# Layer-norm statistics of five stages taken in the tail of the stage ahead, in a one-core transformer kernel

## The reference

```
x = x + L0_xattn(_layernorm(x), ctx, ...)   # a0: 32 heads, position bias, own rms norm
x = x + L0_ffn(_layernorm(x), ...)          # f0: 512x512 base, 8 LoRA experts with a sparsemax router
x = x + L1_xattn(_layernorm(x), ctx, ...)   # a1: attention inside patches, 8 heads
x = x + L1_ffn(_layernorm(x), ...)          # int8 matmul, done inside stage a2
x = x + L2_xattn(_layernorm(x), ctx, ...)   # a2: 32 query, 8 key heads, rotary positions
x = x + L2_ffn(_layernorm(x), ...)          # f2: gated, 1376 wide, weights rounded to 4-bit codes
x = x + L3_xattn(_layernorm(x), ctx, ...)   # a3: keys from context and x, normed queries and keys
x = x + L3_ffn(_layernorm(x), ...)          # f3: 64 experts of rank 8, best 16 of them
```

## Time and profile before

| | us |
|---|---|
| median of 3 runs (3140.70 to 3143.68) | 3140.89 |
| the profiled execution | 3129.63 |
| its span, first to last instruction | 3127.9 |
| first VectorE instruction of f0 | 905.84 |
| of a1 | 988.94 |
| of f2 | 1894.89 |
| of a3 | 2112.50 |
| of f3 | 3012.56 |

### The profile page before, as it was taken

How to read it: one execution, slowest core, us unless ns; L and a number is a source line. 1 busy time by engine, 2 the same in 40 slices (tenths; PEclk the granted TensorE clock), 3 DMA queues, 4 the chain that set the end, 5 groups by cost and what they waited for, 6 DMA issues and landing times. The chain is left out here.

```text
span 3127.9 us, 44736 instructions
## 1 busy us (share of the span) xinstructions
PE 2876.8 (92%) x16404; PEld 2478.2 (79%) x16404; DVE 1994.3 (64%) x3493; ACT 1376.1 (44%) x3393; POOL 1322.3 (42%) x1178
## 2 busy tenths in 40 slices
PE   7999999999876886969999998998999999999967
PEld 6888888888765764758888886877999999999946
DVE  5777777778765787878988875345444444444453
ACT  3656556565521553234444432214434444443520
POOL 6455535544422653455555540004434434343420
PEclk9999999999987997989999999999999999999978
DMA  4112112112121002011111103101000101000000
GB/s 134 46 58 64 59 44 64 60 50 65 39 82 46 11 4 65 27 40 43 40 41 41 39 21 115 41 11 41 28 18 28 28 18 29 27 28 18 17 28 27
DMA packets 77832, 131.85 MB, mean 42 GB/s; under 512 B 10025, under 2 KB 23601, under 8 KB 77233
## 3 DMA queue, kind: packets, MB, share of 16 engines
q1 hardware_dynamic: 68112, 112.10, 11.7%
q10 hardware_dynamic: 9504, 16.91, 1.7%
HBM read 114.23 MB, written 14.75 MB: 41 GB/s over the span
## 5 line engine op out<-in xcount | busy, mean ns | idle before, releaser
L89 PE MATMUL a_pa<-a_wo,a_ot 128*128 128x512 f32 x2304 | 538.1, 391 | 9.6 <-issue 7.5
L89 PEld LDWEIGHTS a_pa<-a_wo,a_ot 128*128 128x128 f32 x2304 | 429.7, 188 | 104.6 <-issue 13.0
L362 DVE SCALAR_TENSOR_TENSOR a_nf_acc<-a_nf_t,a_nf_acc 128x512 f32<-128x512 bf16 (+1 forms) x462 | 403.1, 873 | 42.4 <-ACT a_nf_t L316 11.4
L316 ACT ACTIVATE a_nf_t<-a_nf_w,a_nf_shifts 128x512 bf16<-128x512 f32 (+1 forms) x495 | 321.7, 709 | 202.8 <-DVE a_nf_w L346 173.1
L89 PE MATMUL a_pa<-h_t,a_wqk 128*128 128x512 f32 x1536 | 373.7, 396 | 1.7 <-DVE h_t L773 1.7
L89 PEld LDWEIGHTS a_pa<-h_t,a_wqk 128*128 128x128 f32 x1536 | 282.3, 189 | 56.5 <-DVE h_t L773 1.9
L89 PE MATMUL a_pa<-a_wv,ctx_t 128*128 128x512 f32 x960 | 234.0, 400 | 30.6 <-POOL a_wv L532 15.7
L89 PE MATMUL a_pa<-ctx_t,a_wqk 128*128 128x512 f32 x960 | 227.5, 393 | 21.5 <-POOL a_wqk L1651 21.2
L89 PEld LDWEIGHTS a_pa<-a_wv,ctx_t 128*128 128x128 f32 x960 | 181.4, 192 | 68.6 <-POOL a_wv L1651 15.7
L89 PEld LDWEIGHTS a_pa<-ctx_t,a_wqk 128*128 128x128 f32 x960 | 181.7, 190 | 61.0 <-POOL a_wqk L1651 23.2
L1009 POOL TENSOR_TENSOR a_prob<-a_prob,a_inv 128x512 f32<-128x512 f32 x128 | 130.4, 1040 | 181.1 <-DVE a_inv L1375 181.1
(11 more groups left out here) (356 smaller groups left out, 6008.5 us busy)
## 6 DMA issues: line engine op xcount, KB each, us to landing
a_raw<-in_a_w SPq DMA_DIRECT2D x288, 256.0 KB, 2.6
a_nf_w<-in_nf ACTq DMA_DIRECT2D x32, 256.0 KB, 2.7
nf_rounded<-a_nf_acc ACTq DMA_DIRECT2D x32, 256.0 KB, 2.0
f_rows<-nf_rounded SPq DMA_DIRECT2D x22, 256.0 KB, 2.9
ctx_kept<-ctx_t SPq DMA_DIRECT2D x1, 4096.0 KB, 17.2
ctx_t<-ctx_kept SPq DMA_DIRECT2D x1, 4096.0 KB
f_cols<-nf_rounded SPq DMA_DIRECT2D x11, 256.0 KB, 3.7
a_ctx_raw<-in_ctxt SPq DMA_DIRECT2D x4, 512.0 KB, 6.5
```

Of the source, the lines that this page charges most:

```text
L89: ins = nc.tensor.matmul(out, lhs(a), rhs(b), start=first and i == 0, stop=last and i == 2)
L316: self.nc.scalar.activation(self.t[:, m % NF4_RING, cols], self.w[:, p % 2, cols], ACT.Identity, bias=self.shifts[:, u - 2:u - 1], scale=s ...
L362: ins = nc.vector.scalar_tensor_tensor(acc, t, c, acc, inner, outer)
```

## The change

The norms of f0, a1, f2, a3 and f3 become `CarriedNorm`s that outlive a stage: their statistics, variances and powers lie in one small buffer outside the stages, their semaphores in a stage `carry` that is closed behind the store. In the last stretch of the stage ahead, after the last sum into batch b, VectorE takes the statistics of batch b - 1; after batch 4 it aggregates batches 0 to 3, and GpSimd takes their power at the end of its own work. So a stage starts with batches 0 to 3 ready to be normed and the statistics of batch 7, then the aggregates and power of batches 4 to 7, left.

In `TransposedNorm` the low part of batch b - 3 follows the norming of batch b. GpSimd's large splits in f0 and f3 wait until all eight batches are normed. In f2 four batches are normed, then the weight chunk is turned on VectorE, then normings and low parts alternate. In a1 the two normings come first, the weights' high part waits for its own two transfers only, and TensorE starts on the first half of `w_split`. In a2 three small buffers and a statistics buffer move into another stage buffer's place.

```diff
+class CarriedNorm(Norm):
+    def take_on_vector(self, nc, b, x):
+        nc.vector.bn_stats(self.stats[:, b, :], x[:, b, :]).then_inc(self.own, 1)
+
+    def half_on_vector(self, nc, dve, g):
+        bs = slice(4 * g, 4 * g + 4)
+        dve.wait_ge(self.own, 8 * g + 4)
+        for b in range(4 * g, 4 * g + 4):
+            nc.vector.bn_aggr(self.mv[:, b, :], self.stats[:, b, :]).then_inc(self.own, 1)
+        dve.wait_ge(self.own, 8 * g + 8)
+        nc.vector.tensor_scalar(self.var[:, bs], self.mv[:, bs, 1], 1e-5, None, ALU.add).then_inc(self.var_ready, 1)
+
+    def half_on_gpsimd(self, nc, pool, g):
+        bs = slice(4 * g, 4 * g + 4)
+        pool.wait_ge(self.half_set, 1)
+        pool.wait_ge(self.var_ready, g + 1)
+        nc.gpsimd.tensor_tensor(self.rstd[:, bs], self.var[:, bs], self.half[:, bs], ALU.pow).then_inc(self.rstd_ready, 1)
...
 class TransposedNorm:
     def on_vector(self, dve):
...
         dve.wait_ge(norm.rstd_ready, 1)
+        norm.apply(nc, 0, h[:, 0, :], x).then_inc(self.h_ready, 1)
+        norm.take_on_vector(nc, NB - 1, x)
+        norm.half_on_vector(nc, dve, 1)
+        for b in range(1, NB):
+            if b == 4:
+                dve.wait_ge(norm.rstd_ready, 2)
+            norm.apply(nc, b, h[:, b, :], x).then_inc(self.h_ready, 1)
+            if b >= 3:
+                low(b - 3)
+        for b in range(NB - 3, NB):
+            low(b)
...
 # tail of a0 (of a2, a3, f0 and f2 likewise)
                 nc.vector.tensor_tensor(x[:, b, :], bank(key), x[:, b, :], ALU.add).then_inc(added, 1)
+                if n == H // 2 - 1 and b > 0:
+                    dve.wait_ge(added, added_count["o", n, b - 1])
+                    ahead.take_on_vector(nc, b - 1, x)
+                    if b == 4:
+                        ahead.half_on_vector(nc, dve, 0)
...
 # a3, VectorE
-            norm.stats_on_vector(nc, Steps(dve, own_norm), x)
             dve.wait_ge(norm.rstd_ready, 1)
             for b in range(NB):
+                if b == 1:
+                    norm.take_on_vector(nc, NB - 1, x)
+                    norm.half_on_vector(nc, dve, 1)
+                if b == 4:
+                    dve.wait_ge(norm.rstd_ready, 2)
                 norm.apply(nc, b, hn[:, b, :], x).then_inc(h_ready, 1)
...
 # f0, GpSimd
             pool.wait_ge(loaded, 48)
+            pool.wait_ge(norm.h_ready, NB)
...
 # f3, GpSimd
             norm.on_gpsimd(pool)
+            pool.wait_ge(norm.h_ready, NB)
...
 # a1, VectorE
-            norm.stats_on_vector(nc, Steps(dve, own_norm), x)
...
+            dve.wait_ge(norm.rstd_ready, 1)
+            apply(0)
+            apply(1)
+            norm.take_on_vector(nc, NB - 1, x)
+            norm.half_on_vector(nc, dve, 1)
+            dve.wait_ge(w_hi, 1)
+            nc.vector.tensor_tensor(w[:, LO, :], raw_w[:, :], w[:, HI, :].bitcast(F32), ALU.subtract).then_inc(w_split, 1)
...
 # a1, TensorE
-            pe.wait_ge(w_split, 2)
+            pe.wait_ge(w_split, 1)
...
 # a1, ScalarE
-            act.wait_ge(w_loaded, 16 * SMALL_LOADS)
+            act.wait_ge(proj_loaded, 32)
             nc.scalar.activation(w[:, HI, :], raw_w[:, :], ACT.Copy).then_inc(w_hi, 1)
+            split_h(0)
+            split_h(1)
+            act.wait_ge(small_loaded, 16 * SMALL_LOADS)
...
 # f2, VectorE
-            norm.stats_on_vector(nc, Steps(dve, norm_own), x)
-            turn(0, range(3))
...
+            norm.take_on_vector(nc, NB - 1, x)
+            norm.half_on_vector(nc, dve, 1)
+            dve.wait_ge(norm.rstd_ready, 1)
+            for b in range(4):
+                norm.apply(nc, b, norm_h[:, b, :], x).then_inc(h_ready, 1)
+            turn(0, range(3))
+            dve.wait_ge(norm.rstd_ready, 2)
+            for b in range(4, NB):
+                norm.apply(nc, b, norm_h[:, b, :], x).then_inc(h_ready, 1)
+                rest_of_h(b - 4)
+            for b in range(4, NB):
+                rest_of_h(b)
...
 # program
         store_stage(nc, x, out)
+        carry.close()
```

More of the change, by code:

```diff
@@ L134, with __init__ @@
 class TransposedNorm:
-    def __init__(self, nc, st, x, ident, h_t, banks, space, h, lnw_in=None, h2=None, sq=None):
-        self.nc, self.x, self.ident, self.h_t, self.lnw_in, self.h, self.h2, self.sq = nc, x, ident, h_t, lnw_in, h, h2, sq
+    def __init__(self, nc, st, norm, x, ident, h_t, banks, h):
+        self.nc, self.x, self.ident, self.h_t, self.h = nc, x, ident, h_t, h
         self.tp = [bank.rearrange("p (c n) -> p c n", c=DC) for bank in banks]
[L144 to L158, removed]
-    def on_gpsimd(self, pool):
[L161 to L166, removed]
@@ L587, in _ @@
                     split(("k", h + 3))
+            ahead.set_half(nc)
+            ahead.half_on_gpsimd(nc, pool, 0)
         @block.tensor
@@ L901, in latent_tiles, with latent_attention_stage @@
     return order
-def latent_attention_stage(nc, x, ident, ctx_t, h_t, free_at, pieces_in, kq_norm_in):
+def latent_attention_stage(nc, x, ident, ctx_t, h_t, free_at, pieces_in, kq_norm_in, norm, ahead):
     st = Stage(nc, "a3")
@@ L1999, in add_output @@
                 nc.vector.tensor_tensor(x[:, b, :], bank(key), x[:, b, :], ALU.add).then_inc(a_taken, 1)
+                if n == H // 2 - 1 and b > 0:
+                    dve.wait_ge(a_taken, taken_count["o", n, b - 1])
+                    ahead.take_on_vector(nc, b - 1, x)
+                    if b == 4:
+                        ahead.half_on_vector(nc, dve, 0)
             norm_steps = Steps(dve, own_norm)
@@ L2787, with ffn2_stage @@
 FF_GROUPS = (HC2 + 1) // 2
-def ffn2_stage(nc, x, ident, h_t, rounded, ctx_t, ctx_kept):
+def ffn2_stage(nc, x, ident, h_t, rounded, ctx_t, ctx_kept, norm, ahead):
     st = Stage(nc, "f2")
@@ L2850, in _ @@
         def _(pool):
-            norm.set_half(nc)
-            norm.rstd_on_gpsimd(nc, pool)
+            norm.half_on_gpsimd(nc, pool, 1)
+            ahead.half_on_gpsimd(nc, pool, 0)
         @block.tensor
@@ L2989, in add, with rest_of_h @@
                 nc.vector.tensor_tensor(x[:, b, :], pd[:, d % 2, :], x[:, b, :], ALU.add).then_inc(d_used, 1)
-            norm.stats_on_vector(nc, Steps(dve, norm_own), x)
-            turn(0, range(3))
-            dve.wait_ge(norm.rstd_ready, 1)
-            for b in range(NB):
-                norm.apply(nc, b, norm_h[:, b, :], x).then_inc(h_ready, 1)
-            for b in range(NB):
+                if group == FF_GROUPS - 1 and b > 0:
+                    dve.wait_ge(d_used, d)
+                    ahead.take_on_vector(nc, b - 1, x)
+                    if b == 4:
+                        ahead.half_on_vector(nc, dve, 0)
+            def rest_of_h(b):
                 dve.wait_ge(h_hi, b + 1)
@@ L3250, in program @@
         ident = sb("ident", [P, P])
+        carry = Stage(nc, "carry")
+        carry_space, half_set = sb("carry_space", [P, 11 * NB]), carry.sem("half_was_set")
+        norms = {n: CarriedNorm(carry, carry_space, f"{n}_", half_set) for n in ("f0", "a1", "f2", "a3", "f3")}
         ctx_at = nc.sbuf_base
```

166 lines of the change are left out of this document (65 added, 101 removed).

## The result

| kernel | median of timed executions, us | ratio to the kernel before, 95% interval |
|---|---|---|
| before | 3140.8 (3137.3 to 3143.7) | |
| changed | 3118.1 (3116.6 to 3120.5) | 0.9929 (0.9912 to 0.9946) |
| changed, run again beside 19 executions of before (3138.5) | 3121.1 (3114.9 to 3125.6) | 0.9944 (0.9927 to 0.9962) |

The profiled execution of the changed kernel took 3116.6 us with a span of 3114.7, 13.2 less than the profiled one of before. The forecast was 3132.4 with a range of 3119.5 to 3141.5: the sign was right, the gain was more than twice as large.

What follows compares the result with a forecast made beforehand. TensorE, busy 92%, was taken as the bound, with gains only at seams between stages. Terms -5.3 - 6.7 - 1.1 + 3.3 + 0.6 + 0.75 = -8.45 gave 3121.2 profiled, 3132.4 as median; range 3119.5 to 3141.5.

Steps and rivals of the forecast that it cites:

- I carry the difference over: Whole kernel: the median's 11.3 us above the profiled execution of before is added to 3121.2, giving 3132.4.
- the good case: f0: weights land at S+10.24, after the last norming at S+8.3; TensorE starts at S+14.05 instead of 20.02, term -5.3.
- I take the first: f3: GpSimd's next split gets in behind every tiny VectorE instruction; TensorE at S+22.1 instead of 29.41, term -6.7.
- Rival 1: f3: pairs of casts and subtractions pass together, 4.5 us more gain, -12.9 in all, 3128.0; chance 0.17.
- a3's tail: End of a3: statistics moved between last sums fit, only the statistic of batch 6 sticks out, +0.65.
- f2's tail: Last sums of f2: with statistics a batch costs 1.20 instead of 0.91 us, +2.9.
- f2's start: f2: transposes need not wait for the first norming; gate matmuls at S+14.8 instead of 16.57, -1.1 including the tail's +0.65.
- the end: End of the kernel: one more clearing of semaphores and barrier, +0.75, bounds 0.3 and 1.36.
- the wait for the mask: a1: placing keys waits for the mask, so an earlier TensorE start gains nothing; a1's term is +0.6.
- Rival 2: f0 and f3: no collision counts, f0 -7.1 and f3 -17.1, together -20.7, 3120.2; chance 0.12.
- Rival 3: Gains eaten: f0's subtraction caught (-2.4), needing earlier weights or later low parts; f2 gains nothing; -2.9, 3138.0; chance 0.16.
- Rival 4: First 24 matmuls of f2, a3 and f3 stay at 1.2 GHz, +17; net +8.7, 3149.6; chance 0.10.

## Why the forecast was wrong

It was 14.3 us too high. Two steps failed: how VectorE and GpSimd take turns in f3, and carrying one execution's distance from the median over to another kernel. By terms, forecast minus measured:

- **The median, 9.8.** "I carry the difference over": the profiled execution of before lay 11.3 us under its median, that of the changed kernel 1.5 (3.8 when it was run again). The five profiled executions of before took 3129.6, 3138.1, 3134.9, 3129.5 and 3134.3: I had one of the two lowest. One cause is shown: in two of five f0's weights land up to 1.4 us earlier and a long split holds a norming for 5.4. I costed f0 against the good case; in the changed kernel the normings are over before any landing, and that gain, 2.2 us on average, was in no term. Another is a3, up to 4 us with the granted clock, in either kernel. All executions of before lie between 3129.5 and 3144.7; that the median of the timed ones lies 4 us above that of the profiled ones stays unexplained.
- **f3, 6.2.** The step "I take the first": that GpSimd's next split gets in behind every tiny instruction, which put TensorE's start at S+22.1. It was S+16.2. In the changed kernel the router's cast and its subtraction were held, and the keys' cast and subtraction passed with them in 0.17 and 0.21 us: two instructions caught, not three, worth 4.5 us. Four variants that keep the wait show the same; in two kernels of this study (before with the wait, and the changed one without) three were caught. The earlier trace rows showed that a turn can be lost, not that it always is. Rival 1, pairs that pass together, had this mechanism right: it gave S+17.6. Of the other 1.7 us, 1.4 are an earlier start (the last norming is over at S+7.35 and not 8.3, as the power held none, and the hand-overs were shorter), and 0.3 are a3's tail, later by 0.36 and not 0.65.
- **f0, 1.7.** The size was near and the order of events was not as forecast: the norm phase, over 1.1 us sooner, let the cast in ahead of the first split, and only the subtraction was held. That is 1.35 us; the other 0.3 are again the tail, 0.35 for 0.65.
- **a3, f2, a1, end.** f2's tail +2.7 for +2.9, a3's start +0.40 for +0.4, f2's start -1.74 for -1.1, the end +0.47 for +0.75: right mechanisms and sizes. In a1 I had the wait for the mask right and missed 1.1 us, the placing of keys by two engines released at once. These terms together are off by 0.4.
- **In the other direction, 3.5** of the profiled span were lost elsewhere, 3.85 of it in a3's body, which the second profile did not repeat.

9.8 + 6.2 + 1.7 + 0.4 less 3.5 is 14.6; 0.2 of it is time around the spans, 1.7 us before and 1.9 after. What the change is worth, estimated from the stretches, is 16.7 us and the 2.2 of f0's average: 18.9. Both measured intervals, 17.0 to 27.6 and 11.9 to 22.9 us, contain it, so part of the first 23 us may be the luck of four executions a kernel. Rival 2 (no collision) was wrong as a mechanism, since casts and subtractions were held, and that its time of 3120.2 was the closest is luck. Rival 3 named the right danger in the wrong kernel: the landing that is 1.3 us earlier hurts before, not after. Rival 4 did not happen.

Of the change's parts: the GpSimd wait by itself is worth 9 us in the kernel before by the medians (4.8 in f3 and on average 1.5 in f0 by the stretches) and nothing in the changed one by the medians, the early statistics 13 us, and those of a3 cost 2.7. The Trainium skill (VectorE: DVE Perf Modes, section The DRAIN you can't avoid) lets an instruction start when the pipe is empty, by which the pair of sum and statistic would take 1.37 us, but the same section says that one that is not held starts earlier, which the prediction left out; the tail of f2 shows 1.20, the second case. Another page of the Trainium skill (SBUF — State Buffer, section Who interferes with whom) has the one that issues first keep the port for a whole instruction; the trace agrees with every tiny instruction held in f3, over within 0.1 us of the other's end. Where both next ones start within 0.01 us of each other that rule leaves the order open, and the order was worth 4.5 us from there to TensorE's start (3028.38 to 3030.66 in the changed kernel, 3034.99 to 3041.77 in before with both waits).

**Open.** Who gets the port when both wait. It repeated in every profiled execution of the same program (31.3 us in five, 18.4 in two), did not change when the cast came 2.4 us later, and differed between programs that differ in one wait. No run here tells why.

## What to carry to other kernels

Where two engines share a port, put the short work that somebody waits for ahead of the long instructions that nobody waits for, by the order in the queue or by one wait; don't bet on who wins. Before a sum of terms is trusted, take several profiles: a transfer that lands 1 us sooner can move a stage by 5. Work that is moved into the stage ahead is cheap only where that stage's tail has idle time on the engine: it cost 0.4 us each in a0 and a3, and 2.7 in f2.

## What the runs showed of the hardware

- A tiny VectorE instruction beside a long GpSimd one ends with it, whatever its own length: 4.20, 4.19, 4.51 and 1.80 us for instructions of 0.17 to 0.23.
- Low parts with one operand in PSUM were not held beside splits (1.27 to 1.41 us for two), nor statistics and aggregates beside clears. Normings, casts and subtractions from SBUF to SBUF were held by splits (a norming 1.80 us, a cast 4.20, a subtraction 4.51). A clear held normings (7.47 us for two) and the addition of 1e-5 (2.54), but not the subtraction of `a_w`, 0.76 us in the middle of one.
- Placing keys took 7.81 to 7.83 us on VectorE where GpSimd started 0.01 us ahead of it, and 6.70 where VectorE started 0.14 us ahead.
- The granted clock at the start of a3 differs between executions of the same program (0.91 and 0.97 or 0.98 over 70 us, in both kernels), and a3 is 3.5 to 4 us longer at the lower one.
